# The product of the weighted values and the inverse softmax sums moves from GpSimd to VectorE, behind the reciprocal, and all queues are ordered anew

## The reference, cut to what matters

```python
x = x + xattn(layernorm(x), ctx)          # 8 heads of 16 channels, rope on 8 of the 16
x = x + ffn(layernorm(x))                 # 512 -> 2048 -> 512, ternary weights
# xattn: scores = q k^T / 4; p = softmax(scores); out = p v; Wo out + bo
# ffn:   silu(bitlinear(x, w_gate)) * bitlinear(x, w_up), then a Hadamard transform
#        over 2048, act_quant to 8 bits, and the ternary w_down
# act_quant: scale = 128 / max|x|; round(x * scale) clipped to [-128, 127]; / scale
```

## Time and profile before

| | us |
|---|---|
| median of 3 executions | 1508.82 |
| the profiled execution's own time | 1509.78 |
| its span, first to last instruction | 1508.0 |
| PE busy | 1414.5 (94%) |
| DVE busy | 1229.5 (82%) |
| ACT busy | 1168.6 (77%) |
| POOL busy | 1069.9 (71%) |
| mean granted TensorE clock | 0.975 |

### The profile page before, as it was taken

One profiled execution on the slowest core, in us unless ns is written; L12 is line 12 of the kernel. 1 busy time (PEld: TensorE's weight loads), 2 busy tenths in 40 slices (PEclk: granted clock), 3 DMA queues, 4 the chain that ended last, 5 costly groups with the idle time before them and its releaser, 6 DMA issues.

```text
span 1508.0 us, 31029 instructions
## 1 busy us (share of the span) xinstructions
PE 1414.5 (94%) x11042; PEld 743.4 (49%) x11042; DVE 1229.5 (82%) x2149; ACT 1168.6 (77%) x2033; POOL 1069.9 (71%) x803
## 2 busy tenths in 40 slices
PE   2678999999999999999999999999999999999985
PEld 1214455455555544555555445555555455555443
DVE  2757788888888888888888888988888888888744
ACT  4586778888788888887788788877887888877663
POOL 3122788777777788777777887777778877777662
PEclk9677999999999999999999999999999999999998
DMA  8852344333344443323434433323344433333000
GB/s 211 225 116 46 58 72 77 62 65 62 61 74 68 78 78 64 66 62 60 77 64 78 78 64 71 60 64 69 64 78 78 72 64 63 64 52 64 16 8 15
DMA packets 81113, 108.13 MB, mean 72 GB/s; under 512 B 9664, under 2 KB 59200, under 8 KB 79936
## 3 DMA queue, kind: packets, MB, share of 16 engines
q1 hardware_dynamic: 77744, 93.56, 34.6%
q10 hardware_dynamic: 3216, 12.58, 2.4%
HBM read 38.73 MB, written 8.39 MB: 31 GB/s over the span
## 4 chain that ended last, share of the span: by engine, by line
PE 79%; ACT 9%; DVE 4%; DMA 3%; issue 3%; SPq 1%; POOL 1%; POOLq 0%; ACTq 0%; DVEq 0%
PE pv L495 15%; PE ring L536 14%; PE s L480 13%; PE s L454 13%; PE ring L574 7%; PE ring L550 6%; PE ring L428 4%; ACT region L726 4%; PE ring L504 2%; PE ring L442 2%; DMA region<-parts 2%; PE ring L561 1%; ACT parts L821 1%; ACT xqT L735 1%; ACT y_last L769 1%
## 5 line engine op out<-in xcount | busy, mean ns | idle before, releaser
L1035 DVE TENSOR_REDUCE maxima<-s 128x1 bf16<-128x512 f32 x1024 | 671.1, 683 | 110.4 <-PE s L454 107.8
L726 ACT ACTIVATE region<-s 128x512 f32<-128x512 f32 x1024 | 570.4, 594 | 101.0 <-PE s L480 93.0
L454 PE MATMUL s<-region 96*128 96x512 bf16 x1024 | 369.3, 390 | 26.2 <-DVE maxima L1035 13.5
L1293 POOL TENSOR_TENSOR region<-region,th 128x512 f32<-128x512 f32 x126 | 158.9, 1273 | 293.8 <-DVE th L1130 292.1
L480 PE MATMUL s<-region 97*128 97x512 bf16 x1024 | 357.8, 384 | 7.6 <-ACT region L726 4.0
L495 PE MATMUL pv<-region,v_ext 128*17 128x512 f32 x2048 | 264.2, 599 | 0.0
L292 POOL TENSOR_TENSOR region<-region 128x512 f32<-128x512 f32 x189 | 240.6, 1273 | 12.5
L293 POOL TENSOR_TENSOR region<-region 128x512 f32<-128x512 f32 x189 | 241.1, 1275 | 0.0
L454 PEld LDWEIGHTS s<-region 96*128 96x128 bf16 x1024 | 95.0, 98 | 207.3 <-DVE maxima L1035 110.9
L480 PEld LDWEIGHTS s<-region 97*128 97x128 bf16 x1024 | 91.0, 98 | 172.7 <-ACT region L726 140.0
L290 POOL TENSOR_TENSOR region<-region 128x1024 f32<-128x1024 f32 x63 | 148.0, 2371 | 3.4 <-DVE region L293 3.4
(11 more groups left out here) (111 smaller groups left out, 1862.5 us busy)
## 6 DMA issues: line engine op xcount, KB each, us to landing
region<-parts SPq DMA_DIRECT2D x384, 128.0 KB, 4.3
x_in<-in_x SPq DMA_DIRECT2D x32, 256.0 KB, 2.7
c_in<-in_ctx SPq DMA_DIRECT2D x32, 256.0 KB, 3.0
rope_c<-region SPq DMA_DIRECT2D x64, 128.0 KB, 2.3
x_res<-in_x SPq DMA_DIRECT2D x32, 256.0 KB, 2.9
out<-o_sb SPq DMA_DIRECT2D x32, 256.0 KB, 4.7
region<-in_wg_t ACTq DMA_DIRECT2D x1, 2048.0 KB, 8.9
region<-in_wu_t ACTq DMA_DIRECT2D x1, 2048.0 KB, 7.6
```

The costliest lines, as they stand in the source:

```text
L454: pe.matmul(s1[p][:, :], q_stack[k][0:STACK, h, 128 * c:128 * (c + 1)], k_stack[k][0:STACK, h, :], start=True, stop=True).then_inc(s1_full ...
L726: act.activation(probs[:, n % 8, :], s2[n % 2][:, :], ACT.Exp, scale=SCALE).then_inc(exp_done, 1)
L1035: dve.reduce_max(maxima[:, c, h:h + 1], s1[p][:, :], AXX).then_inc(s1_max[p], 1)
L1293: pool.tensor_tensor(zj, zj, th[:, j % 2, :], ALU.mult).then_inc(glu_done, 1)
```

## The change

`mix` goes from POOL's list. Its multiplication is now the last instruction of `normalise` on DVE: it waits for the reciprocal and, for g = 0, for the `turn_back` of the batch before. The lists of PE, ACT, DVE and SP, and `RING` with them, are in a new order; a few calls change the step in which they stand with no change of batch. POOL's list keeps its order without the two `mix` calls.

```diff
@@ normalise (DVE)
                 dve.reciprocal(inv_sum[:, :], blocks[:, :, DH]).then_inc(inv_done, 1)
+                dve.wait_ge(inv_done, 2 * b + g + 1)
+                if g == 0:
+                    wait(dve, attn_done, b)
+                dve.tensor_tensor(mixed[:, :].rearrange("p (n g e) -> p n g e", g=2, e=DH)[:, :, g, :],
+                                  blocks[:, :, 0:DH], inv_sum[:, :].unsqueeze(2).to_broadcast([128, 16, DH]),
+                                  ALU.mult).then_inc(mixed_done, 1)
@@ POOL
-            def mix(b, g):
...
@@ POOL step
                 hadamard_half(t - 2, 1)
-                mix(t - 1, 0)
                 third_part(t + 1)
-                mix(t - 1, 1)
                 hadamard_last(t - 2, 0)
@@ DVE step (one place of many)
-                half_gates(t - 2, 0)
-                half_gates(t - 2, 1)
-                round_piece(t - 2, 2, 7)
-                glu(t - 2, 0)
...
+                half_gates(t - 2, 0)
+                round_piece(t - 2, 2, 4)
+                reduce_scores(t, 3)
+                half_gates(t - 2, 1)
+                round_piece(t - 2, 2, 5)
+                round_piece(t - 1, 1, 3)
+                reduce_scores(t, 4)
+                glu(t - 2, 0)
@@ ACT step (one place of many)
-                gate_rows_out(t - 1)
-                xqT_out(t - 1)
-                exps(t, 0)
-                exps(t, 1)
...
+                xqT_out(t - 2)
+                exps(t - 1, 0)
+                exps(t - 1, 1)
+                gate_rows_out(t - 2)
```

More of the change, by code:

```diff
@@ L601, in step @@
                 scores(t - 2, 27)
-                y_transpose(t - 4, 1)
                 score_max(t - 1, 25)
@@ L665, in step @@
                 scores(t - 1, 13)
+                score_max(t, 12)
+                gate_up(t - 2, "gate", 3)
                 scores(t - 1, 14)
-                gate_up(t - 2, "gate", 3)
+                score_max(t, 13)
                 scores(t - 1, 15)
-                score_max(t, 12)
+                weigh(t - 1, 2)
+                score_max(t, 14)
                 scores(t - 1, 16)
-                weigh(t - 1, 2)
-                score_max(t, 13)
-                score_max(t, 14)
+                score_max(t, 15)
@@ L674, in step @@
+                gate_up(t - 2, "up", 3)
                 scores(t - 1, 17)
-                gate_up(t - 2, "up", 3)
-                gate_sum(t + 1)
-                score_max(t, 15)
+                score_max(t, 16)
                 scores(t - 1, 18)
```

315 lines of the change are left out of this document (152 added, 163 removed).

## The result

The changed kernel takes 1695.62 us (median of 4, 1691.77 to 1696.25), the kernel before 1509.86 beside it: a ratio of 1.1225, 95% interval 1.1197 to 1.1253. The forecast of slower was right, its size of 18 us is a tenth of the 186 us lost, and the time lies far outside the range.

The account below looks back on a forecast made before the run. PE was taken to set the pace (busy 428.00 of 430 us). 30 batches x (0.9 - 0.3) = 18 us, plus 1 at the start, on 1509.8 gave 1528.8, or 1528 us against the median; range 1498 to 1546 us.

Parts of the forecast that it names:

- Price beside GpSimd: Each product on DVE costs the rest of POOL's running instruction plus 0.3 us, between 0.42 and 2.6 us.
- The place: The first product of a batch asks during POOL's `rest`, with 1.4 us of it left; wait taken as 1.0 us.
- +0.9 us a batch reach PE: The first product's 1.0 us wait delays reduction 26, its `score_max` and the last two `weigh`: PE 0.9 us late.
- the likeliest case: Whole kernel, first product waiting 0.5 to 1.4 us: 1516 to 1542 us, forecast 1528, chance 0.45.
- The two are in balance when the product costs 0.42 us, with 0.1 to spare: Before the last two `weigh`: DVE finishes reduction 26 at 724.0, PE could begin at 724.28.
- the new order gives 0.3: At `gate_up`, PE waits less for `xqT_out` in the new lists: 0.3 us a batch gained, range 0 to 0.6.
- a product that hides: Rival: the first product meets a POOL gap or instruction's end, or PE has slack; 1501 us, faster, chance 0.30.
- The second product costs nothing: Behind the last `weigh`, before `attn_out`: wait of 0 to 2.3 us, up to 1.2 covered; nothing taken.
- The start, +1 us: First batch: the fourth absolute sum of gate weights stands ahead of `second_part`; +1 us, from -3 to +4.
- The rivals: Product hides, 1501 us, 0.30; loss and gain cancel, 1509 us, 0.14; both products wait, 1552 us, 0.11.
- both products waiting: Rival: the second product also meets a fresh `hadamard_last`, PE waits 0.8 us more at `attn_out`; 1552 us, chance 0.11.

Follow-up runs that it names:

- `turn` over 128: Changed kernel with GpSimd's 64-partition addition `turn` made over all 128 partitions from the second batch on: 1582.52 us, ratio 1.0481.
- one gap: Changed kernel with one more GpSimd wait, for its own end, behind `rest`: 1586.67 us, ratio 1.0496.
- the PSUM version: Changed kernel with the reciprocal written to PSUM, so the product reads one SBUF operand; the next `weigh` waits for the product: 1523.07 us, ratio 1.0081.
- the two PSUM versions: Product on VectorE with its inverse sums in PSUM, once in the new orders (1523.07 us), once in the orders of the kernel before (1535.55 us).
- the order alone: Changed kernel with the product back on GpSimd in its old places, all new orders kept: 1525.62 us, ratio 1.0099.
- the run with gaps behind the gate products and `rest`: Changed kernel with GpSimd waits for its own end behind gate products 2 and 3 and behind `rest`: 1532.18 us, ratio 1.0142.
- the last probe: Separate program: GpSimd's first addition over 16 to 128 partitions, then six short ones, VectorE's product beside them; products ended 8.72 to 8.73, 8.32 us, or at next hand-over.

## Why the prediction was wrong, step by step

- *Price beside GpSimd, "the rest of POOL's running instruction and 0.3 us of its own", at most 2.6 us.* This step failed. It holds wherever GpSimd had stood still since its last 64-partition instruction, and with `turn` over 128 (the product ends 0.28 us behind the instruction). In the changed kernel the product waited past two hand-overs, 4.3 us in place of my 1.0. The earlier trace rows showed the hand-over of one pair and said nothing of a GpSimd that goes on without a stop; the earlier trace rows did show the 64x1024 row of `turn` and the gapless run behind it. The Trainium skill (SBUF — State Buffer, "SBUF: two separate sides") calls the port pair an exclusive lock; the traces agree with full blocking (the 0.42 us product took 4.70). It leaves open who gets it next.
- *How much of the miss that is.* Without it, in the run with `turn` over 128, the kernel takes 1582.52 us, still above my range. So 113 us of the miss are this step, and the 55 us from 1528 to 1582 lie in the terms below, the place, the order and the second product.
- *The place.* Right: inside `rest`, 0.15 us after its start. But I had 0.7 us after it, by the sum of two estimates, so that even under the rule the wait is 1.86 us, not 1.0.
- *"+0.9 us a batch reach PE".* The mechanism is right, the slack was mis-sized: of 4.28 us of wait PE was idle for 3.54, of 1.86 us (one gap) for 1.10, so some 0.7 us were covered and not 0.1. And I left the clock out. Behind 3.5 us of idle PE it was granted 0.50 for 3.4 or 6.8 us, 1.7 or 3.0 us a batch, some 70 us in all. With one gap, and 1.1 us of idle PE, this doesn't happen: clock 1.00 in the stretch.
- *The range of the likeliest case, 1516 to 1542.* It forgets the 0.1 us to spare that the sum itself uses; by the same terms it is 1513 to 1540.
- *"The two are in balance when the product costs 0.42 us, with 0.1 to spare", and "the new order gives 0.3".* Together they promised 1501 us for a product that hides; the PSUM version took 1523.07. Its batch is 0.54 us longer than before, without a wait of PE for the product, so the order lost where I had a gain. The 0.31 us that it gains between the two PSUM versions are in part the removal of that experiment's own wait of 0.57; with the product on GpSimd the order costs 0.64. The wait at `gate_up` in the earlier trace rows shrank, and came back as PE waiting for `quant_x`, seen here in the PSUM version (the order alone shows the same 0.32). First the row of the kernel before that precedes L536, then the PSUM version:

```profile
738.24 0.38 PE L480 MATMUL s<-region 97*128 97x512 bf16 x1
```

```profile
740.94 0.38 PE L454 MATMUL s<-region 96*128 96x512 bf16 x1
741.64 0.38 PE L512 MATMUL ring<-eye_b,xq 128*128 128x128 bf16 x4 [0.32 <-DVE xq L1113]
...
742.31 0.60 PE L454 MATMUL s<-region 96*128 96x512 bf16 x2
742.89 1.05 PE L536 MATMUL ring<-xqT,wg 128*128 128x128 bf16 x16
```

  Before, one L480 of 0.22 us took 0.53 up to L536 (738.77): 0.31 us lost. Here one L454 of 0.22 us takes 0.70, and two before L536 take 0.58: some 0.62 us lost. That is 0.3 of the 0.54 us; the rest was not traced to one wait.
- *The second product costs nothing, "up to 1.2" of wait being covered.* Right in the changed kernel, where it takes 0.42 us. In the run with gaps behind the gate products and `rest` it alone waited, for 1.14 us, and the batch was 43.60 against 43.42: nearly covered, as forecast. With one gap it waited 1.8 us, beside `hadamard_last` (L290). There the batch is 2.1 us longer than in the PSUM version and PE's stall behind the first product is 1.1, which leaves some 1.0 us for the second and all else.
- *The start, +1 us.* In the run with the orders alone the fourth batch's first product began at 252.6 us, and at 253.7 before: no loss, and too small to matter.
- *The rivals.* None came true; the worst that I had priced, both products waiting, gave 1552. No rival had a product that waits past a hand-over.

## What to carry to other kernels

Before an instruction with two SBUF operands goes to VectorE, look in GpSimd's timeline for instructions that leave a group of 16 partitions idle (16, 64 and 112 partitions did it here, 120 did not), and for its next standstill behind the request: the wait can reach that far. A wait of GpSimd for its own semaphore costs 0.08 us and let VectorE in, ahead of the request (1584.39 us) or behind it (1586.67); one operand in PSUM removes the question. Price PE's idle time with the clock that follows it.

## What was unexpected of the hardware

- A GpSimd instruction that leaves a group of 16 partitions idle keeps VectorE's two-input SBUF instruction out of the later hand-overs: 8.7 us after the chain's start instead of the next hand-over with 112 partitions against 120, and 4.70 us against 2.28 in the kernel. The cause, cores that run ahead, forecast the 18 products of the last probe; the single cores are in no trace.
- TensorE's granted clock fell to 0.50 (1.2 GHz) behind 3.5 us of idle time, for 3.4 us in some batches and 6.8 in others with the same idle time, in a steady part that otherwise has 1.00. Behind 1.1 us of idle time it did not fall.
- VectorE in between two instructions costs GpSimd some 0.17 us (L293 1.44 instead of 1.27), less than the product's 0.42.
